# Fused patch embedding, linear attention and routed experts: a third patch slot, bias rows split on GpSimd, earlier expert splits, part of V's bias on TensorE, and a drain interleaved with tiles

## What is computed

```python
h = concat([patch_embed(x), txt], axis=1)
n = layernorm(h)
Q, K = elu(n @ Wq.T + bq) + 1, elu(n @ Wk.T + bk) + 1
V = n @ Wv.T + bv                                    # 16 heads of 16
h = h + (Q @ (K.T @ V) / (Q @ sum(K))) @ Wo.T + bo   # per head
n = layernorm(h)
e, w = argmax(n @ gate_w.T), sigmoid(max(n @ gate_w.T))
h = h + expert_e(w * n)                              # 8 experts, 256 -> 128 -> 256
```

## Time and profile before

| | us |
|---|---|
| three executions | 504.41, 505.61, 505.67 (median 505.61) |
| the profiled execution, whole | 504.4 |
| its span in the trace | 502.6 |
| PE busy | 450.9 |
| DVE busy | 394.9 |
| POOL busy | 282.1 |
| ACT busy | 257.6 |

### The profile page before, as it was taken

How to read it: one execution, slowest core, us unless ns; L and a number is a source line. 1 busy time by engine, 2 the same in 40 slices (tenths; PEclk the granted TensorE clock), 3 DMA queues, 4 the chain that set the end, 5 groups by cost and what they waited for, 6 DMA issues and landing times. The chain is left out here.

```text
span 502.6 us, 12361 instructions
## 1 busy us (share of the span) xinstructions
PE 450.9 (90%) x3692; PEld 434.5 (86%) x3692; DVE 394.9 (79%) x1298; ACT 257.6 (51%) x688; POOL 282.1 (56%) x676
## 2 busy tenths in 40 slices
PE   4997999999999999999999999899569989788872
PEld 4997999999999999999999998889558878678861
DVE  4559678999999999998998999898738667576651
ACT  4443464544635545446545544453427667666640
POOL 0001213587777777777776775666466545555553
PEclk9998999999999999999999999999959999999995
DMA  8763121223111182111111121046416772211120
GB/s 290 250 213 111 37 53 54 61 61 83 51 54 45 33 262 88 47 50 34 44 54 34 34 62 45 21 108 179 132 41 191 236 208 74 75 56 65 67 69 12
DMA packets 35099, 46.27 MB, mean 92 GB/s; under 512 B 8951, under 2 KB 27114, under 8 KB 35035
## 3 DMA queue, kind: packets, MB, share of 16 engines
q1 hardware_dynamic: 25818, 30.37, 20.3%
q0 software_dynamic: 9216, 15.12, 9.8%
HBM read 26.73 MB, written 17.17 MB: 87 GB/s over the span
## 5 line engine op out<-in xcount | busy, mean ns | idle before, releaser
L684 POOL DMA_INDIRECT out<-result,rows_all x64 | 62.6, 979 | 51.5 <-issue 29.3
L646 POOL DMA_INDIRECT sorted_rows<-rows,place x64 | 76.7, 1198 | 22.2 <-issue 12.0
L760 ACT ACTIVATE den<-b_att,z_eps 114x32 f32<-114x32 f32 x32 | 9.2, 287 | 95.0 <-PE b_att L1428 82.3
L777 ACT ACTIVATE q_exp<-b_w,bq_s 128x228 f32<-128x228 f32 x64 | 28.9, 451 | 38.2 <-PE b_w L1320 37.3
L590 POOL TENSOR_SCALAR ve<-mv 114x2 f32<-114x2 f32 x32 | 7.4, 233 | 69.6 <-DVE mv L945 66.9
L1318 PE MATMUL b_w<-xnT_hi,wq_hi 128*128 128x256 f32 x128 | 38.8, 303 | 6.0 <-DVE logits L1023 5.9
L1318 PE MATMUL b_kg<-wkgv_hi,xnT_hi 128*114 128x264 f32 x128 | 41.9, 327 | 0.0
L1318 PE MATMUL b_w<-wo_hi,attnT_hi 128*114 128x264 f32 x124 | 40.5, 327 | 0.0
L1231 DVE TENSOR_TENSOR act_u<-b_kg,silu_g 128x128 f32<-128x128 f32 x64 | 18.5, 289 | 27.7 <-ACT silu_g L849 19.6
L863 ACT ACTIVATE xs<-rows_all 128x256 f32<-128x256 f32 x64 | 39.4, 618 | 0.0
L1318 PE MATMUL b_kg<-wgu_hi,xsT_hi 128*128 x128 | 37.1, 290 | 2.1 <-DVE xsT_lo L887 1.2
(11 more groups left out here) (242 smaller groups left out, 1826.1 us busy)
## 6 DMA issues: line engine op xcount, KB each, us to landing
rows_all<-sorted_rows SPq DMA_DIRECT2D x64, 130.0 KB
rows_all<-in_x SPq DMA_DIRECT2D x18, 384.0 KB, 4.0
rows_all<-in_txt SPq DMA_DIRECT2D x32, 154.0 KB
rows_all<-in_wgu SPq DMA_DIRECT2D x8, 256.0 KB
rows_all<-patch_out SPq DMA_DIRECT2D x48, 36.0 KB
sorted_rows<-tail_rows SPq DMA_DIRECT2D x9, 130.0 KB
sorted_rows<-rows,place POOLq DMA_INDIRECT x64
rows_all<-in_wdown SPq DMA_DIRECT2D x8, 128.0 KB
```

The costliest lines, as they stand in the source:

```text
L646: G.indirect_dma_start(out=scratch[0:EXPERTS * REGION, :], out_offset=bass.IndirectOffsetOnAxis(ap=place[:, k, b:b + 1], axis=0), in_=rows ...
L684: G.indirect_dma_start(out=out, out_offset=bass.IndirectOffsetOnAxis(ap=rows_all[:, t.n, ID:ID + 1].bitcast(I32), axis=0), in_=result[:, k ...
L760: S.activation(den[:].rearrange("p b (k h) -> p b k h", k=KC), heads[:, :, :, P:KVW], ACT.Identity, bias=z_eps[0:TOK, :]).then_inc(den_don ...
L777: S.activation(q_exp[:, c, :], at, ACT.Exp, bias=bq_s[:, c:c + 1])
```

## The change

- The ring of split patch units has three slots in place of two.
- The bias rows (now with V's bias) are three row DMAs issued by ACT at the start, into an 112-row tile that POOL clears; POOL splits them by columns in chains of small steps: K and V first, then the output bias, then the eight gate columns once DVE has made them. DVE keeps two copies of `gate_columns`.
- Each expert's weights are loaded for itself between the text loads (n = 8 to 18), split by ACT in steps 8 to 19 and by DVE one step later.
- In pairs 9 to 20 and 26 to 31 V's bias is put into PE by two more bf16 matmuls, and ACT copies V out of PSUM in DVE's place.
- The drain's lists and the first tile steps are interleaved on all four engines; a tile's first transposes come ahead of `apply(31)`, the last scatter behind the stores of tiles 1 to 4.

```diff
-BIAS_O, BIAS_K, BIAS_W = 0, KGW, 2 * KGW
-BIAS_ROWS, BIAS_R = (0, 32, 64), 80
+BIAS_O, BIAS_K, BIAS_V, BIAS_W = 0, KGW, 2 * KGW, 2 * KGW + D
+BIAS_ROWS, BIAS_ONE, BIAS_R = (0, 64, 96), 32, 112
+X_RING = 3
...
-            xp_hi, xp_lo = parts("xp", [P, 2, FC, P], room)
+            xp_hi, xp_lo = parts("xp", [P, X_RING, FC, P], room)
...
+        def v_by_pe(p):
+
+            return 9 <= p <= 20 or p >= 26
+
...
-        s_expert_w = sem("s_expert_w")
+        s_expert_w = [sem(f"s_expert_w{e}") for e in range(EXPERTS)]
...
         EXPERT_LOAD = 16
-        DRAIN_B, STEPS_B = 5, range(5, TILES + 3)
-        GU_STEP, DOWN_STEP = 17, 25
-        EXPERTS_AT = 18
+        STEPS_B = range(7, TILES + 3)
+        GU_STEPS, DOWN_STEPS = (8, 9, 11, 12, 14, 15, 17, 18), (10, 13, 16, 19)
 
...
+            def load_expert(e):
+
+                at, end = e * (GU + DOWN), (e + 1) * (GU + DOWN)
+                sp.wait_ge(h2_ready, (end - 1) // (2 * ROW) + 1)
+                sp.dma_start(expert_raw[:, at:at + GU], wgu[:, e * GU:(e + 1) * GU]).then_inc(s_expert_w[e], 16)
+                sp.dma_start(expert_raw[:, at + GU:end], wdown[:, e * DOWN:(e + 1) * DOWN]).then_inc(s_expert_w[e], 16)
...
-            sp.dma_start(bias_s[:], bias).then_inc(s_weights, 16)
...
-            for n in range(6, EXPERTS_AT):
+            for n in range(6, PAIRS):
                 if n < len(ROW_SETS):
                     patch_rows(n)
-                load_text(n)
-            sp.wait_ge(h2_ready, RAW_PAIRS)
-            for e in range(EXPERTS):
-                at = e * (GU + DOWN)
-                sp.dma_start(expert_raw[:, at:at + GU], wgu[:, e * GU:(e + 1) * GU]).then_inc(s_expert_w, 16)
-                sp.dma_start(expert_raw[:, at + GU:at + GU + DOWN], wdown[:, e * DOWN:(e + 1) * DOWN]).then_inc(s_expert_w, 16)
-            for n in range(EXPERTS_AT, PAIRS):
+                if n in GU_STEPS:
+                    load_expert(GU_STEPS.index(n))
                 load_text(n)
 
...
+            done = [0]
+
+            def bias_link(ins):
+
+                ins.then_inc(bias_step, 1)
+                done[0] += 1
+                pool.wait_ge(bias_step, done[0])
+
+            def bias_parts(columns):
+
+                for r, first in enumerate(BIAS_ROWS):
+                    below = slice(first, BIAS_R)
+                    whole, part = bias_s[below, columns], bias_bf[below, columns]
+                    bias_link(G.tensor_copy(part, whole))
+                    if r < 2:
+                        rest = slice(BIAS_ROWS[r + 1], BIAS_R)
+                        bias_link(G.tensor_tensor(bias_s[rest, columns], bias_s[rest, columns], bias_bf[rest, columns], ALU.subtract))
+
+            bias_link(G.memset(bias_s[:], 0.0))
+            bias_link(G.memset(bias_bf[BIAS_ROWS[1]:], 0.0))
+            bias_link(G.memset(bias_s[BIAS_ONE:BIAS_ONE + 1, BIAS_K:BIAS_K + D], 1.0))
+            pool.wait_ge(s_bias, 16 * len(BIAS_ROWS))
+            bias_parts(slice(BIAS_K, BIAS_W))
+            bias_parts(slice(0, D))
+            pool.wait_ge(bo_gate_ready, 1)
+            bias_parts(slice(D, BIAS_K))
             step(-2)
             step(-1)
             pool.wait_ge(s_const, 16 * CONST_DMAS)
...
             for i in range(PAIRS + 1):
                 step(i)
-            count_chosen(PAIRS - 2)
-            rstd2_of(PAIRS - 2)
-            top_value(PAIRS - 2)
-            scatter(PAIRS - 3)
-            rstd2_of(PAIRS - 1)
-            count_chosen(PAIRS - 1)
-            top_value(PAIRS - 1)
-            scatter(PAIRS - 2)
-            scatter(PAIRS - 1)
-
...
-            straight(range(0, DRAIN_B), tile_step)
+            count_chosen(PAIRS - 2)
+            scatter(PAIRS - 3)
+            rstd2_of(PAIRS - 2)
+            top_value(PAIRS - 2)
+            count_chosen(PAIRS - 1)
+            tile_step(Turn(0, 2))
+            scatter(PAIRS - 2)
+            rstd2_of(PAIRS - 1)
+            top_value(PAIRS - 1)
+            straight(range(3, 7), tile_step)
+            scatter(PAIRS - 1)
             straight(STEPS_B, tile_step)
...
-                if u.had(2):
-                    act.wait_ge(unit_done, u.upto(2))
-                S.copy(xp_hi[:, u.slot(2)].rearrange("p f n -> p (f n)"), x_in[:, k * X_UNIT:(k + 1) * X_UNIT]).then_inc(x_hi_ready, 1)
+                if u.had(X_RING):
+                    act.wait_ge(unit_done, u.upto(X_RING))
+                S.copy(xp_hi[:, u.slot(X_RING)].rearrange("p f n -> p (f n)"), x_in[:, k * X_UNIT:(k + 1) * X_UNIT]).then_inc(x_hi_ready, 1)
...
-                act.wait_ge(s_expert_w, 32 * EXPERTS)
+                act.wait_ge(s_expert_w[e], 32)
...
                 for e in (2 * n, 2 * n + 1):
+                    act.wait_ge(s_expert_w[e], 32)
...
+            def values(p):
+
+                act.wait_ge(kvp_done, p + 1)
+                act.wait_ge(kvm_done, p)
+                S.copy(v_sb[:, :, :, 0:P].rearrange("p b k e -> p (b k) e"),
+                       b_v[0:TOK, :].rearrange("p (a e) -> p a e", e=P)).then_inc(v_ready, 1)
 
...
-                if GU_STEP <= i < GU_STEP + EXPERTS:
-                    gate_up_high(i - GU_STEP)
-                if DOWN_STEP <= i < DOWN_STEP + EXPERTS // 2:
-                    down_high(i - DOWN_STEP)
+                if i in GU_STEPS:
+                    gate_up_high(GU_STEPS.index(i))
+                if i in DOWN_STEPS:
+                    down_high(DOWN_STEPS.index(i))
                 if 0 <= i:
                     keys(i)
+                    if v_by_pe(i):
+                        values(i)
...
+            act.wait_ge(bias_step, 1)
+            for row in BIAS_ROWS:
+                act.dma_start(bias_s[row:row + 1, :], bias).then_inc(s_bias, 16)
             w_tok_part(0, s_tokw)
...
             attention_high(PAIRS - 2)
             S.activation(silu_ahead[:], bq_s[:, 0:1], ACT.Silu)
-            tile_step(Turn(0, -4))
-            tile_step(Turn(0, -3))
+            straight(range(-4, -1), tile_step)
+            denominators(PAIRS - 1)
+            tile_step(Turn(0, -1))
             tanh(PAIRS - 4)
-            denominators(PAIRS - 1)
+            tile_step(Turn(0, 0))
+            attention_high(PAIRS - 1)
+            straight(range(1, 3), tile_step)
             tanh(PAIRS - 3)
-            attention_high(PAIRS - 1)
+            straight(range(3, 5), tile_step)
             tanh(PAIRS - 2)
-            straight(range(-2, 0), tile_step)
+            straight(range(5, 7), tile_step)
             tanh(PAIRS - 1)
-            straight(range(0, DRAIN_B), tile_step)
             straight(STEPS_B, tile_step)
...
-                if GU_STEP < i <= GU_STEP + EXPERTS:
-                    gate_up_low(i - GU_STEP - 1)
-                if DOWN_STEP < i <= DOWN_STEP + EXPERTS // 2:
-                    down_low(i - DOWN_STEP - 1)
+                if i - 1 in GU_STEPS:
+                    gate_up_low(GU_STEPS.index(i - 1))
+                if i - 1 in DOWN_STEPS:
+                    down_low(DOWN_STEPS.index(i - 1))
                 if 0 <= i - 3:
                     route(i - 3)
                 if 0 <= i:
                     keys(i)
-                    values(i)
...
+                dve.wait_ge(s_bias, 16 * len(BIAS_ROWS))
                 V.tensor_copy(wo_gate, wo_gates.rearrange("p (k e) -> p k e", k=KC)).then_inc(gate_step, 1)
-                V.tensor_copy(bias_s[:, BIAS_O + D:BIAS_K], bo_gate).then_inc(bias_step, 1)
...
-                V.tensor_copy(bias_bf[third], bias_s[third]).then_inc(bias_step, 1)
+                V.tensor_copy(bias_s[:, BIAS_O + D:BIAS_K], bo_gate).then_inc(bo_gate_ready, 1)
...
             queries(PAIRS - 1)
+            tile_step(Turn(0, -2))
             route(PAIRS - 3)
             attention(PAIRS - 1)
             residual(PAIRS - 2)
             gate_logits(PAIRS - 2)
+            straight(range(-1, 1), tile_step)
+            places(PAIRS - 3)
             route(PAIRS - 2)
-            stats_2(PAIRS - 2)
             attention_low(PAIRS - 1)
-            places(PAIRS - 3)
+            straight(range(1, 3), tile_step)
             residual(PAIRS - 1)
             gate_logits(PAIRS - 1)
             places(PAIRS - 2)
+            stats_2(PAIRS - 2)
+            tile_step(Turn(0, 3))
             route(PAIRS - 1)
-            straight(range(-2, 0), tile_step)
+            tile_step(Turn(0, 4))
             stats_2(PAIRS - 1)
+            tile_step(Turn(0, 5))
             places(PAIRS - 1)
             late_count()
-            straight(range(0, 2), tile_step)
+            tile_step(Turn(0, 6))
+            tile_step(Turn(0, 7))
             late_slots()
-            straight(range(2, 4), tile_step)
+            tile_step(Turn(0, 8))
             late_rows()
-            straight(range(4, 7), tile_step)
-            straight(range(7, TILES + 3), tile_step)
+            straight(range(9, TILES + 3), tile_step)
...
                     pe.wait_ge(place_ready, p)
+                if p == PAIRS - 2:
```

(30 more changed lines are left out.)

31 lines of the change are left out of this document (9 added, 22 removed).

## The result

The changed kernel takes 496.65 us (median of 4 runs, 496.36 to 498.15) against 505.38 us (4 runs, 504.41 to 505.67): ratio 0.9866, 95% interval 0.9823 to 0.9908. That ratio is not the quotient of the two medians, which is 0.9827; both lie in the interval, and they stand for gains of 6.8 and 8.7 us. The forecast was 491.7, a gain of 13.7 us. The measured time lies in the range, just above rival (b), "the drain gives nothing", at 495.7.

A forecast was written before the change was run, and what follows sets the result against it. PE was taken to bound the kernel, losing time in a patch-stage hole, slow later pairs and the drain. 504.4 - 4.3 - 5.2 - 4.0 = 490.9 us, plus 0.8, gave 491.7 us; range 486.5 to 497.5.

The forecast's parts named there:

- rival (b): Drain: nothing gained, as POOL's list, with stores ahead of the last scatter, holds `result` every fourth tile; 495.7 us, chance 0.10.
- Patches: Patch stage: moving the bias chain off DVE closes PE's hole near 43 us; net -4.3 us.
- the wait of 3.20 us: Patch stage: PE's wait for `xp_lo` of unit 12, to be won whole, 3.20 us.
- the half clock: Patch stage: PE's slow matmuls after its wait for `xp_lo`, 2.91 us where 1.5 would do; 1.4 us to win.
- The 0.3 us for a later start: Kernel start: ACT's three DMA issues may delay the first weights by nothing to 1.3 us; 0.3 us taken as loss.
- Rival (d): Kernel start: POOL's wide steps block DVE's first low parts, PE starting about 1 us later; 492.7 us, chance 0.05.
- Pairs, -5.2: Pairs 3 to 31: 9.5 us to be had by relieving DVE, less 4.3 us for V's bias matmuls on PE.
- the early table: Late pairs, steps 27 to 29: extra DVE work, expected covered by the 0.68 us DVE saves on V.
- Rival (c): Pair stage: steps with a split stay DVE-bound at 9.63 us, costing 3.2 us; 494.9 us, chance 0.05.
- Drain, -4.0: Drain: interleaved lists bring `result` of tile 9 to 392.5 us against 396.71, 4.2 us won; net -4.0 us.
- Rival (e): Drain: PE's clock falls at a wait and stays at 1.2 GHz, making twelve tiles slower; 509.7 us, chance 0.05.
- Rival (a): Drain gives 3 us more, as ACT's tanh and POOL come earlier and the half clock goes; 488.7 us, chance 0.14.

The follow-up runs named there:

- e2: The kernel before with only the four interleaved drain lists added: 504.84 us, ratio 1.0002 to the kernel before.
- e16: The changed kernel with the bias split back on DVE, POOL only clearing the rows, three patch slots kept: 499.44 us, ratio 0.9914 to the kernel before.
- e7: The changed kernel with POOL's wide bias steps begun only after the fourth patch unit is stored: 476.46 us, beside 477.56 for the changed kernel.
- e15: The changed kernel with V's bias put through PE by matmul in all 32 pairs: 497.70 us, ratio 0.9879 to the kernel before.
- e14: The changed kernel with V's bias added by DVE in all pairs, no bias matmul for V: 500.54 us, ratio 0.9916 to the kernel before.
- e9: The changed kernel, unaltered, run again on a chip with the short tile stage: 476.99 us, ratio 0.9792 to the kernel before.
- e10: The changed kernel with the old drain lists, on a chip with the short tile stage: 476.80 us, ratio 0.9797 to the kernel before.
- e6: The changed kernel with eight result buffers in place of four: 472.22 us, ratio 0.9675 to the kernel before.
- e11: The changed kernel with the old drain lists and eight result buffers: 477.13 us, ratio 0.9787 to the kernel before.
- e12: The changed kernel with eight result buffers, tile 0's transposes behind apply(31), ACT's tanh steps moved and a later last scatter: 468.31 us, ratio 0.9613 to the kernel before.
- e3: The changed kernel with ACT's tanh of pair 28 moved earlier, right behind the row scaling of tiles 0 and 1: 495.11 us, ratio 0.9818 to the kernel before.
- e4: The changed kernel with tile 0's transposes, copy and low part behind apply(31): 494.70 us, ratio 0.9816 to the kernel before.
- e1: The changed kernel with the four drain lists of the kernel before: 493.73 us, ratio 0.9799 to the kernel before.

## Why the prediction was wrong: its sum, term by term

**Patches, -4.3: right in size.** The profiled pair of executions shows 6.5 us (60.86 to 54.40), but single executions spread at the start (e2 has 58.96 with the same patch stage). Undoing only the chain costs 3.3 us (e16); against e2 the stage gained 4.4. That the size came out is partly luck: of its parts, the wait of 3.20 us is borne out, while the half clock, put at 1.4 us, was worth 0.7 at the first pair in the execution that had it, and nothing in e2. The 0.3 us for a later start can't be read from one pair of traces (9.27 to 9.66, where the same code starts between 7.88 and 9.77). Rival (d) was right as a mechanism (e7), and its price at the end is below what one execution can tell.

**Pairs, -5.2: 0.8 us too much.** 264.99 us became 260.55, 4.4 won. The price of 0.24 us a pair for two bias matmuls holds (e15: 2.44 us for 11 pairs, 0.22 each), and so does what V would have cost on DVE (e14: 4.3 us more). The excess lies in the early table, which the forecast put at nothing once V had left DVE. Marked by PE's first matmul for a pair's keys, the steps before pairs 27 to 29 take 9.60, 9.65 and 9.95 us where I had 9.36, 1.1 us in all; PE stands still for only 0.36 us between pairs 25 and 30, and what lengthens these steps no run here tests. Of this, 0.24 us comes back because pair 31 pays for its bias behind its exponential, so that 17 of the 18 pairs count. The steps before pairs 10 to 21 take 9.34 to 9.37 us, as forecast. (By the exponential the step before pair 8 seems to take 9.53 us and that before pair 20 only 8.93; PE has 9.19 and 9.35 there, as ACT's expert split stands ahead of the exponential and shifts the mark.) Rival (c) fell: 9.35 and not 9.63.

**Drain, -4.0: nothing. This is the step that failed.** Measured: 3.1 us lost from pair 31 on in the profiled pair, nothing in e2 (1.0002) and in e9 against e10 (476.99 and 476.80). The forecast took `result` 9 as what the end hangs on, and only the store of tile 5 ahead of it; of the store of tile 1 it said that DVE's wait there "may take a little". That wait was the decisive one. I had added up POOL's work as one sum (15.0 + 3.5 + 1.0 + 6.5 us), and not asked what stands ahead of each store. The store of tile 1 was issued 10 us behind its result; `result` 5 came 6 us behind `result` 4, and PE, waiting 2.50 us, fell to half clock (the stretch at 0.82 above). That the wait for the buffers held the new lists back is shown by e6 (eight buffers, 5.3 us faster) beside e11 (eight buffers and the old lists, nothing). After the stall the tiles ran at 2.2 to 3.3 us a step up to `result` 9, not at DVE's 1.2: `result` 9 came 48.6 us behind pair 31, as before (396.71 - 347.87 = 48.8), where I had 44.6. The store of tile 5 was 44.3 us behind pair 31 (381.22), against my 41.5.

So rival (b) describes the outcome: with the drain at nothing and the pairs at -4.4 the prediction's own sum is 504.4 - 4.3 - 4.4 + 0.8 = 496.5 us, against 496.65. That it comes so near is luck: the profiled pair adds up otherwise (6.5 won in the patches, 4.4 in the pairs, 3.1 lost behind them), and the ratio of 0.9866 would be 498.6 us. Its wording, "holds `result` at every fourth tile", is the mechanism. I had argued against it only by its chance of 0.10, though I had written down what spoke for it: 26 us of work for POOL in 27 us. Rival (e) fell: the clock dropped in the drain's waits (0.94, 0.82 and 0.94 in the three windows above) and came back each time. Rival (a) describes what e12 reached, not by POOL being early but by DVE no longer depending on it.

**What stays open.** Whether the new lists cost something on chips with the long tile stage. The old lists have not run beside the changed kernel on such a chip. From the exponential of pair 31 to the end of the span, the seven traces there with the changed lists, or nearly so (the changed kernel, e2, e3, e4, e14, e15, e16), have 157.7 to 159.4 us, the two with the old ones (the kernel before, e1) 154.7 and 156.4. On the others the changed kernel has 137.5 to 138.3 us in three traces and the old lists 137.2 in e10. That speaks for a loss of one microsecond or more on the long kind. The times do not decide it: e3 and e4 are 1.4 and 1.0 us above e1 on their chip, within the intervals, and e2 has 1.0002. A gain of 4 us is excluded on either kind. Open too is what of the changed kernel's gain is kept there: its ratio was 0.9866 (0.9823 to 0.9908), on the other kind 0.9788 to 0.9792 in three runs.

## What to carry to other kernels

When tiles are started ahead of a drain, follow the buffer that comes free last, not the sum of work of the engine that frees it: here a ring of four with its stores behind a scatter gave back all that the early start won, and doubling the ring (4 KB a partition) was worth 5.3 us on top of lists that alone were worth nothing. A gain read from one execution is worth only what a second one confirms. Mark a stage by the engine that bounds it: another engine's instruction shifts with what stands ahead of it. Set a ratio only against one from the same chip.
